# Two up blocks ahead of the q sums and the router in a fused attention and expert kernel

## The chip, the cores and the metric

The kernel runs on one core of a Trainium2 chip. The metric is the device time of one launch in microseconds (us), median of the runs; lower is better.

## The reference

A transformer block over 32 batch elements of 256 tokens, width 256, in float32. First comes attention with 4 heads of 64: queries from the normalized tokens, keys and values from the tokens and 77 context rows, so 333 keys. Then comes a mixture of experts on the result, with a shared part of inner width 512 and 8 experts of inner width 128, of which a router picks two per token.

```python
x = x + attention(ctx, layernorm(x), mask)     # q and k are divided by their RMS per head
h = layernorm(x)
logits = h @ gate_weight.T                     # sigmoid, bias, best of two groups, top 2 of 8, weights sum to 2.5
routed = sum over experts e of w[t, e] * (relu(h @ up[e].T) ** 2) @ down[e].T
shared = (relu(h @ shared_up.T) ** 2) @ shared_down.T
x = x + routed + shared
```

## The kernel before, in words

Every engine has its program written out by hand, in a function `step(b, experts, following)` that is run for the 32 batch elements; engines meet through semaphores that count up. Step b does the attention of element b and, woven into it, the expert part of element b-1 (`f`), and towards its end it projects k, v and q of element b+1. The first step has no expert part, the last one no next element (`following` is false), and after the loop the expert part of element 31 runs alone.

Precision: a float32 product is made of three float32r matmuls, from a high and a low part of either operand (`split_product`, L295 to L297). So each activation is copied once rounded (hi, mostly ScalarE) and subtracted once (lo, VectorE or GpSimd).

**TensorE** (step from L512 on): `transpose_k` (six transposes, L362), `sum_q_squares` (L349: 32 small matmuls in four column tiles into bank 0 of `attn_ps`), `router` (L465: 32 of the same kind into bank 3 of `attn_ps`), `up` 0 and 1 (L295 to L297, 12 matmuls each), the first two score pairs (L383 to L387, two at a time on half of the rows), `up` 2 and 3, score pairs 2 and 3, the shared down block (24 matmuls), transposes of probabilities 0 to 2 (L397, three each), then expert down blocks, `up` 4 and 5, and further transposes in turn. At the end come the projections of b+1, `down` 6, the four transposes of x2 (L452), and `down` 7.

PSUM has eight banks: four in `attn_ps`, two in `up_ps` (up blocks take turns), two in `down_ps` (shared part and experts take turns). Heads u and u+4 share a bank of `attn_ps`; transposed probabilities 0 to 2 go to banks 0 to 2, so `transpose_probs(b, u)` waits until head u+4 has been masked out of its bank:

```python
if u < PT_RING:
    pe.wait_ge(masked_done, b * U + SCORE_RING + u + 1)
```

**VectorE** in one step: `k_low` twice, statistics of the input of b+1, `mask_scores` of heads 0 to 3 (L906), `negate_max` (L913, 128x4, needs `q_scale`), the first eight levels of the router's choice (L996 to L1017: small operations, each waiting for the one before; `pair_hi` L1003, `top2` L1010, `group_sum` L1012, the two `group_sel` L1015 and L1017), `mask_scores` of heads 4 to 7, further levels, the shared sum (L1058), casts of hidden pairs 3 to 5 (L1052) between the accumulations of the experts (L1067). Near the end: `normalize2` (L968), `k_norms` and `k_normalize` of b+1, `x2_low` (L976), `q_low`, `add(6)`, `q_norms` (L864), `add(7)`.

**ScalarE**: `k_high`, `router_exp` (the exponential of the logits), then `hidden(p)` for up pairs 0 to 2 (relu out of PSUM, square as high part, square as float32), the softmax exponentials, copies out of PSUM; at the end `q_out` (copy and square of q) and `x2_high` (x2 as float32 and as high part).

**GpSimd** in one step, in this order: `q_scales` (a power operation on 128x8), `hidden_low` 0 to 2 (L1268, a 128x512 subtraction of two SBUF tensors each), `rstd_first` (a power operation on 128x3; not in the first and last steps), `residual` (L1242, x_res, a 128x512 addition of two SBUF tensors), `hidden_low` 3 and 4, `ln_low`, `hidden_low` 5, `rstd_second`, `k_scales`.

SP issues the loads of b+2, which wait for x_hat and x_res of b, and the stores.

Of the kernel before, what the change touches and what calls it, by code (L numbers as in the profile page):

```python
# [33 lines left out]
def build(nc, x, ctx_in, mask, vectors, w_q, w_kv, w_out, b_out, gate_t, gate_bias, up_t, down_t, out):  # L34
# [21 lines left out]
    with ExitStack() as stack:  # L56
# [234 lines left out]
        def _(pe):  # L291
# [48 lines left out]
            def sum_q_squares(b, first):  # L340


                pe.wait_ge(q_sq_done, b + 1)
                if first:
                    pe.wait_ge(head_sel_done, 1)
                for t in range(T):
                    for ft in range(FT):
                        for tile in COLUMN_TILES:
                            last = nc.tensor.matmul(attn_ps[tile, 0, t * H + 2 * ft:t * H + 2 * ft + 2],  # L349
                                                    q_sq[:, ft, t * P + tile.start:t * P + tile.stop], head_sel[:],  # L350
                                                    start=True, stop=True)
                last.then_inc(qn_ps, 1)
# [14 lines left out]
            def score_pair(b, pair, experts):  # L367
                t, ft = divmod(pair, FT)
                u = 2 * pair
                cols = slice(t * P, (t + 1) * P)  # L370
                if pair == 0:
                    pe.wait_ge(q_norm_done, b + 1)
                    pe.wait_ge(k_hi_done, (b + 1) * FT)
                    pe.wait_ge(k_lo_done, (b + 1) * FT)
                elif pair == 1:
                    if experts:
                        pe.wait_ge(exp_neg_done, b)
                else:
                    pe.wait_ge(masked_done, b * U + u - 2)
                low, high = slice(0, DH), slice(DH, P)  # L380
                banks = [attn_ps[:, (u + i) % SCORE_RING, 0:KPAD] for i in range(2)]
                for i, rows in enumerate((low, high)):
                    nc.tensor.matmul(banks[i], q_hi[rows, ft, cols], k_hi[rows, ft, :], start=True, stop=False)  # L383
                for i, rows in enumerate((low, high)):
                    nc.tensor.matmul(banks[i], q_hi[rows, ft, cols], k_lo[rows, ft, :], start=False, stop=False)
                for i, rows in enumerate((low, high)):
                    nc.tensor.matmul(banks[i], q_lo[rows, ft, cols], k_hi[rows, ft, :], start=False,  # L387
                                     stop=True).then_inc(score_ps, 1)
# [67 lines left out]
            def router(b, first):  # L456

                if first:
                    pe.wait_ge(gate_in, DMA)
                pe.wait_ge(x2_full_done, (b + 1) * FT)  # L460
                pe.wait_ge(x2_hi_done, (b + 1) * FT)
                for t in range(T):
                    for k in range(FT):
                        for tile in COLUMN_TILES:
                            last = nc.tensor.matmul(attn_ps[tile, 3, t * E:(t + 1) * E],  # L465
                                                    x2_full[:, k, t * P + tile.start:t * P + tile.stop],
                                                    gate_stage[:, k, :], start=k == 0, stop=k == FT - 1)
                last.then_inc(logit_ps, 1)

            def up(b, p, first, following=True):  # L470

                if first and p == 0:
                    pe.wait_ge(w_lo_done, 3 + QUART)
                if p == 0:
                    pe.wait_ge(x2_hi_done, (b + 1) * FT)
                    pe.wait_ge(x2_lo_done, (b + 1) * FT)
                if p == 1 and following:
                    pe.wait_ge(q_lo_done, b + 2)
                if p >= 2 or not first:
                    pe.wait_ge(relu_done, b * PAIRS + p - 1)  # L480
                for j in range(2):
                    for k in range(FT):
                        cols = slice((2 * p + j) * P, (2 * p + j + 1) * P)
                        last = split_product(up_ps[:, (p + 1) % 2, j * S:(j + 1) * S], (up_hi[:, k, cols], up_lo[:, k, cols]),
                                             (x2_hi[:, k, :], x2_lo[:, k, :]), k == 0, k == FT - 1)
                last.then_inc(up_done, 1)
# [6 lines left out]
            def down_shared(b, t, first):  # L493
                if first and t == 0:
                    pe.wait_ge(down_lo_done, QUART)
                if t == 0:
                    pe.wait_ge(*hid_hi_ready(b, SP_PAIRS - 1))
                    pe.wait_ge(hid_lo_done, b * PAIRS + SP_PAIRS)
                    if not first:
                        pe.wait_ge(acc_done, b * ACC)  # L500
                for f in range(FS):
                    last = split_product(down_ps[:, 0, t * D:(t + 1) * D], hidden(f, t),
                                         (down_hi[:, f, :], down_lo[:, f, :]), f == 0, f == FS - 1)
# [3 lines left out]
            def down_expert(b, e, first):  # L507
# [3 lines left out]
                if e > 0:  # L511
                    pe.wait_ge(acc_done, b * ACC + 2 * e - 1)  # L512
                elif not first:
                    pe.wait_ge(acc_done, b * ACC - 2)
                for t in range(T):
# [4 lines left out]
            def step(b, experts, following):  # L520
# [11 lines left out]

                transpose_k(b)
                sum_q_squares(b, first)
                if experts:
                    router(f, f_first)
                ffn("up", 0)
                ffn("up", 1)
                score_pair(b, 0, experts)
# [48 lines left out]
                project_kv(b + 1, 0)  # L588
                project_q(b + 1)
                ffn("down", 6)  # L590
                transpose_x2(b)
                ffn("down", 7)
# [13 lines left out]
            steps(step)  # L606
            router(B - 1, False)
            up(B - 1, 0, False, False)
            up(B - 1, 1, False, False)
            up(B - 1, 2, False)  # L610
            up(B - 1, 3, False)
# [11 lines left out]
        def _(act):  # L623
# [15 lines left out]
            def q_out(b, first):  # L639
# [4 lines left out]
                qv = up_ps[:, 0, :].rearrange("p (f s) -> p f s", f=FT)  # L644
                nc.scalar.activation(q_hi[:], qv, ACT.Copy).then_inc(q_hi_done, 1)
                nc.scalar.activation(q_sq[:], qv, ACT.Square).then_inc(q_sq_done, 1)

# [63 lines left out]
            def router_exp(b, first):  # L711
                act.wait_ge(logit_ps, b + 1)
                if not first:
                    act.wait_ge(router_step, (b - 1) * ROUTER_STEPS + 1)
                nc.scalar.activation(exp_neg[:], attn_ps[:, 3, 0:T * E].rearrange("p (t e) -> p t e", t=T),
                                     ACT.Exp, scale=-1.0).then_inc(exp_neg_done, 1)
# [14 lines left out]
            def step(b, experts, following):  # L731
                first = isinstance(b, int) and b == 0
                f, f_first = b - 1, isinstance(b, int) and b == 1
                ffn = (lambda p: hidden(f, p, f_first)) if experts else (lambda p: None)
                k_high(b, first)
                if experts:
                    router_exp(f, f_first)
                ffn(0)
                if first:
# [29 lines left out]
                if following:  # L769
# [3 lines left out]
                    q_out(b + 1, False)  # L773
                x2_high(b, first)

            act.wait_ge(kv_in, DMA)
# [12 lines left out]
            v_out(0, 1, True)  # L789
            q_out(0, True)  # L790
            for cols in UP_COLS[1:]:
                split_hi(up_hi[:, :, cols], up_stage[:, :, cols])
            steps(step)
            router_exp(B - 1, False)
            hidden(B - 1, 0, False)
            for p in range(1, PAIRS):
# [4 lines left out]
        def _(dve):  # L801
# [57 lines left out]
            def q_norms(b, first):  # L859

                dve.wait_ge(qn_ps, b + 1)
                if not first:
                    dve.wait_ge(q_scale_done, b)
                nc.vector.tensor_scalar(q_norm[:], attn_ps[:, 0, 0:U], DH * RMS_EPS * RMS_EPS, None,  # L864
                                        ALU.max).then_inc(q_norm_done, 1)
# [105 lines left out]

            def x2_low(b):
                for ft in range(FT):
                    dve.wait_ge(x2_full_done, b * FT + ft + 1)
# [104 lines left out]
            def step(b, experts, following):  # L1079
# [15 lines left out]
                k_low(b, 0)  # L1095
                k_low(b, 1)
                if first:
                    normalize1(1, False)
                    up_parts(0)
# [66 lines left out]
                k_norms(b + 1, 1, False)  # L1166
                k_normalize(b + 1, 0, False)
                k_normalize(b + 1, 1, False)
                x2_low(b)
                q_low(b + 1)  # L1170
                add(6)
                q_norms(b + 1, False)
                add(7)

# [25 lines left out]
            q_low(0)  # L1200
            q_norms(0, True)
            dve.wait_ge(gamma_done, 1)
# [18 lines left out]
        def _(pool):  # L1221
# [49 lines left out]
            def step(b, experts, following):  # L1271
                first = isinstance(b, int) and b == 0

                def low(p):
                    if experts:
                        hidden_low(b - 1, p)

                q_scales(b, first)
                if first:
                    for i, rows in enumerate(DOWN_ROWS):  # L1280
                        pool.wait_ge(w_hi_done, 4 + QUART + i)
                        nc.gpsimd.tensor_tensor(down_lo[:, rows, :], down_stage[:, rows, :], down_hi[:, rows, :],
                                                ALU.subtract).then_inc(down_lo_done, 1)
                low(0)
                low(1)
# [75 lines left out]
```

## Time and profile before

| what | value |
|---|---|
| median of 3 runs | 1172.76 us (1172.66 to 1172.81) |
| the profiled execution, its own time | 1171.52 us |
| its span, first to last instruction | 1169.7 us |
| TensorE matmul busy | 1145.7 us (98%) |
| VectorE busy | 1006.4 us (86%) |
| ScalarE busy | 801.6 us (69%) |
| GpSimd busy | 555.2 us (47%) |
| mean granted TensorE clock | 0.993 of full speed |

Busy is the share of the span in which an engine has an instruction in execution. Matmuls overlap, so the starts of two matmuls, not their durations, tell what one costs in a row of them. In the timeline a row gives the start, the duration, engine, line, operation, the tiles written and read, and their sizes; x9 means nine instructions merged, and a bracket at the end tells how long the engine stood idle before the row and for whom. An operation that has begun but is held shows as a long duration, not as idle time.

### The profile page before, as it was taken

Reading aid. Unit: us, or ns where it says so; the run is one execution under the profiler, and the core shown is the slowest. Engines: PE = TensorE matmul, PEld = TensorE weight load, DVE = VectorE, ACT = ScalarE, POOL = GpSimd, SP = SyncE. Lnnn points to the kernel's source line nnn. Section 1 sums busy time; section 2 is a strip of 40 time slices with the busy share of each in tenths; the row PEclk is TensorE's granted clock in tenths of the full one; section 3 lists DMA queues with packets and bytes.
Section 4 is the critical chain, followed back from the end, with each engine's and each line's share of the span. In section 5 each row is a group of like instructions: output and inputs, shape, how many; then the busy total and the mean of one; then the engine's idle time right before and its main releaser. Section 6 shows DMA issues by size and latency. Waiting matters only on the chain. (4 is left out here: it accounts for less than half of the span.)

```text
span 1169.7 us, 32985 instructions
## 1 busy us (share of the span) xinstructions
PE 1145.7 (98%) x11772; PEld 1070.1 (91%) x11772; DVE 1006.4 (86%) x3500; ACT 801.6 (69%) x1900; POOL 555.2 (47%) x473
## 2 busy tenths in 40 slices
PE   7799999999999999999999999999999999999997
PEld 6699999999999999999999999999999999999997
DVE  6688988889888889888899888899888899888877
ACT  5577766677766768766778666678666677666673
POOL 5445444445444445454445454444454444454442
PEclk8899999999999999999999999999999999999999
DMA  5000000000000000000000000000000000000000
GB/s 173 13 14 23 23 22 12 14 23 23 23 12 22 14 23 22 23 11 23 14 22 23 23 11 22 13 23 23 22 11 22 14 23 22 23 10 15 10 11 19
DMA packets 28145, 26.06 MB, mean 22 GB/s; under 512 B 6544, under 2 KB 27440, under 8 KB 27984
## 3 DMA queue, kind: packets, MB, share of 16 engines
q1 hardware_dynamic: 27904, 23.83, 6.5%
q8 instruction: 95, 1.56, 0.6%
q14 instruction: 66, 0.54, 0.2%
q0 software_dynamic: 80, 0.14, 0.1%
HBM read 15.57 MB, written 8.39 MB: 20 GB/s over the span
## 5 line engine op out<-in xcount | busy, mean ns | idle before, releaser
L1268 POOL TENSOR_TENSOR hid_lo<-relu,hid_hi 128x512 fp32r<-128x512 f32 x192 | 248.3, 1293 | 246.6 <-DVE hid_hi L1052 166.2
L295 PE MATMUL down_ps<-down_hi,hid_hi 128*128 128x256 f32 x768 | 233.6, 304 | 1.7 <-ACT hid_hi L726 1.0
L1067 DVE SCALAR_TENSOR_TENSOR acc<-down_ps,route_w,acc 128x256 f32<-128x256 f32 x512 | 222.0, 475 | 8.9 <-PE down_ps L297 8.2
L295 PE MATMUL up_ps<-x_hi,up_hi 128*128 128x256 f32 x768 | 226.8, 295 | 0.0
L297 PE MATMUL down_ps<-down_hi,hid_lo 128*128 128x256 f32 x768 | 215.9, 281 | 0.0
L296 PE MATMUL down_ps<-down_lo,hid_hi 128*128 128x256 f32 x768 | 215.7, 281 | 0.0
L296 PE MATMUL up_ps<-x_lo,up_hi 128*128 128x256 f32 x768 | 214.3, 279 | 0.0
L297 PE MATMUL up_ps<-x_hi,up_lo 128*128 128x256 f32 x768 | 214.2, 279 | 0.0
L676 ACT ACTIVATE probs<-masked,neg_max,q_scale 128x333 f32<-128x333 f32 x256 | 168.1, 658 | 3.4 <-DVE neg_max L913 3.4
L721 ACT ACTIVATE relu_sb<-up_ps 128x512 f32<-128x512 f32 x192 | 113.6, 592 | 72.4 <-PE up_ps L297 69.1
L295 PEld LDWEIGHTS down_ps<-down_hi,hid_hi 128*128 128x128 f32 x768 | 144.4, 188 | 14.2 <-issue 12.9
L295 PEld LDWEIGHTS up_ps<-x_hi,up_hi 128*128 128x128 f32 x768 | 144.0, 188 | 7.3 <-ACT relu_sb L721 6.5
L296 PEld LDWEIGHTS down_ps<-down_lo,hid_hi 128*128 128x128 f32 x768 | 145.2, 189 | 0.0
L297 PEld LDWEIGHTS up_ps<-x_hi,up_lo 128*128 128x128 f32 x768 | 144.4, 188 | 0.0
L297 PEld LDWEIGHTS down_ps<-down_hi,hid_lo 128*128 128x128 f32 x768 | 144.4, 188 | 0.0
L296 PEld LDWEIGHTS up_ps<-x_lo,up_hi 128*128 128x128 f32 x768 | 144.2, 188 | 0.0
L1223 POOL TENSOR_TENSOR rstd<-var,minus_half 128x2 f32<-128x2 f32 (+1 forms) x64 | 49.9, 780 | 167.7 <-DVE var L961 165.7
L683 ACT ACTIVATE up_stage<-attn_ps 111x384 f32<-111x384 f32 x256 | 117.3, 485 | 16.9 <-PE attn_ps L397 16.9
L729 ACT ACTIVATE relu<-relu_sb 128x512 f32<-128x512 f32 x192 | 119.7, 624 | 3.0
L653 ACT ACTIVATE k_sq<-attn_ps 111x512 f32<-111x512 f32 x64 | 31.5, 492 | 125.6 <-PE attn_ps L297 125.6
L906 DVE CUSTOM_DVE_ANT_0 masked<-attn_ps,mask_row 128x333 f32<-128x333 f32 x256 | 114.0, 498 | 2.1 <-issue 2.1
L397 PE MATMUL attn_ps<-ident,probs 128*111 128x128 f32 x768 | 107.7, 277 | 7.0 <-DVE row_max L906 6.9
(145 smaller groups left out, 2851.1 us busy)
## 6 DMA issues: line engine op xcount, KB each, us to landing
out<-acc SPq DMA_DIRECT2D x31, 256.0 KB, 2.2
x_first<-in_x SPq DMA_DIRECT2D x16, 256.0 KB, 2.7
w_stage<-in_x SPq DMA_DIRECT2D x16, 256.0 KB, 2.8
up_stage<-in_up_t SPq DMA_DIRECT2D x1, 1536.0 KB, 6.8
down_stage<-in_down_t SPq DMA_DIRECT2D x1, 1536.0 KB, 8.5
c_first<-in_ctx SPq DMA_DIRECT2D x16, 77.0 KB
w_stage<-in_ctx SPq DMA_DIRECT2D x16, 77.0 KB
w_stage<-in_w_kv SPq DMA_DIRECT2D x1, 512.0 KB, 4.1
```

Of the source, the lines that this page charges most:

```text
L295: nc.tensor.matmul(out_ap, s_hi, m_hi, start=first, stop=False)
L296: nc.tensor.matmul(out_ap, s_hi, m_lo, start=False, stop=False)
L297: return nc.tensor.matmul(out_ap, s_lo, m_hi, start=False, stop=last)
L397: last = nc.tensor.transpose(attn_ps[0:KC, u % PT_RING, c * P:(c + 1) * P], probs[:, u, c * KC:(c + 1) * KC], ident[:])
L676: nc.scalar.activation(probs[:, u, :], masked[:, u, :], ACT.Exp, bias=neg_max[:, u:u + 1], scale=q_scale[:, u:u + 1], accum_out=row_sum[:, ...
L683: nc.scalar.activation(probs_t[:, u % PT_SB, :], attn_ps[0:KC, u % PT_RING, 0:CH * P], ACT.Copy).then_inc(pt_done, 1)
L721: nc.scalar.activation(relu_sb[:, p % 2, :], up_ps[:, (p + 1) % 2, :], ACT.Relu).then_inc(relu_done, 1)
L729: nc.scalar.activation(relu2[:, p % 2, :], relu_sb[:, p % 2, :], ACT.Square).then_inc(relu2_done, 1)
L906: nc.vector.tensor_tensor_reduce(masked[:, u, :], attn_ps[:, u % SCORE_RING, 0:KEYS], mask_row[:], 1.0, -MASKED, ALU.add, ALU.max, row_max ...
L1067: nc.vector.scalar_tensor_tensor(acc[:, t, :], down_ps[:, (e + 1) % 2, t * D:(t + 1) * D], route_w[:, t, e:e + 1], acc[:, t, :], ALU.mult, ...
L1223: nc.gpsimd.tensor_tensor(dst, src, minus_half[0:src.shape[0], 0:src.shape[1]], ALU.pow).then_inc(done, 1)
L1268: nc.gpsimd.tensor_tensor(hid_lo[:, p % HID_RING, :], relu2[:, p % 2, :], hid_hi[:, p % HID_RING, :], ALU.subtract).then_inc(hid_lo_done, 1)
```

## The change

On TensorE, `up` 0 and 1 go ahead of the q sums and the router, so that these two stand directly before score pairs 0 and 1. The q sums now write bank 0 of `down_ps`, the logits bank 1, and both wait until the accumulations of the element before have read those banks. The wait of score pair 0 on `q_norm` goes, and so does that of score pair 1 on `exp_neg`; the shared down block waits for `q_norm` instead and expert 0 for `exp_neg`. The transposes of x2 move ahead of `down` 6. `up` 0 waits for the first half of x2_lo, and for the second half at its fourth matmul.

On ScalarE the square of q moves behind `x2_high`, and `router_exp` behind `hidden(0)`. On VectorE the first half of `x2_low` moves between the two `k_normalize`, and `q_norms` from the end of a step to behind `k_low` of the next. On GpSimd `hidden_low(0)` moves ahead of `q_scales`. The closing stage after the loop takes the same order of router and up blocks. No arithmetic is added or removed.

```diff
@@ sum_q_squares
                 if first:
                     pe.wait_ge(head_sel_done, 1)
+                elif b > 1:
+                    pe.wait_ge(acc_done, (b - 1) * ACC)
...
-                            last = nc.tensor.matmul(attn_ps[tile, 0, t * H + 2 * ft:t * H + 2 * ft + 2],
+                            last = nc.tensor.matmul(down_ps[tile, 0, t * H + 2 * ft:t * H + 2 * ft + 2],
@@ score_pair
                 if pair == 0:
-                    pe.wait_ge(q_norm_done, b + 1)
                     pe.wait_ge(k_hi_done, (b + 1) * FT)
                     pe.wait_ge(k_lo_done, (b + 1) * FT)
-                elif pair == 1:
-                    if experts:
-                        pe.wait_ge(exp_neg_done, b)
-                else:
+                elif pair > 1:
                     pe.wait_ge(masked_done, b * U + u - 2)
@@ router
                 if first:
                     pe.wait_ge(gate_in, DMA)
+                else:
+                    pe.wait_ge(acc_done, b * ACC)
...
-                            last = nc.tensor.matmul(attn_ps[tile, 3, t * E:(t + 1) * E],
+                            last = nc.tensor.matmul(down_ps[tile, 1, t * E:(t + 1) * E],
@@ up
-                    pe.wait_ge(x2_lo_done, (b + 1) * FT)
+                    pe.wait_ge(x2_lo_done, b * FT + 1)
...
+                        if p == 0 and j == 0 and k == 1:
+                            pe.wait_ge(x2_lo_done, (b + 1) * FT)
@@ down_shared
                     if not first:
                         pe.wait_ge(acc_done, b * ACC)
+                    if b + 1 < B:
+                        pe.wait_ge(q_norm_done, b + 2)
@@ down_expert
-                elif not first:
-                    pe.wait_ge(acc_done, b * ACC - 2)
+                else:
+                    pe.wait_ge(exp_neg_done, b + 1)
@@ TensorE step
                 transpose_k(b)
+                ffn("up", 0)
+                ffn("up", 1)
                 sum_q_squares(b, first)
                 if experts:
                     router(f, f_first)
-                ffn("up", 0)
-                ffn("up", 1)
                 score_pair(b, 0, experts)
...
                 project_q(b + 1)
+                transpose_x2(b)
                 ffn("down", 6)
-                transpose_x2(b)
                 ffn("down", 7)
...
-            router(B - 1, False)
             up(B - 1, 0, False, False)
             up(B - 1, 1, False, False)
+            router(B - 1, False)
@@ ScalarE
                 nc.scalar.activation(q_hi[:], qv, ACT.Copy).then_inc(q_hi_done, 1)
+
+            def q_square(b):
+                qv = up_ps[:, 0, :].rearrange("p (f s) -> p f s", f=FT)
                 nc.scalar.activation(q_sq[:], qv, ACT.Square).then_inc(q_sq_done, 1)
...
                 k_high(b, first)
+                ffn(0)
                 if experts:
                     router_exp(f, f_first)
-                ffn(0)
...
                 x2_high(b, first)
+                if following:
+                    q_square(b + 1)
@@ VectorE step
                 k_low(b, 0)
                 k_low(b, 1)
+                q_norms(b, first)
...
                 k_normalize(b + 1, 0, False)
+                x2_low(b, 0)
                 k_normalize(b + 1, 1, False)
-                x2_low(b)
+                x2_low(b, 1)
                 q_low(b + 1)
                 add(6)
-                q_norms(b + 1, False)
                 add(7)
@@ GpSimd step
+                low(0)
                 q_scales(b, first)
...
-                low(0)
                 low(1)
                 low(2)
```

## Rows read from the trace of the kernel before

**Rows 1.** Timeline of TensorE's matmuls, one steady step.

```profile
512.12 0.38 PE L452 MATMUL attn_ps<-ident,x_hat 128*128 128x128 f32 x2
...
513.28 0.75 PE L362 MATMUL attn_ps<-ident,k_rms 111*128 111x111 f32 x6
...
514.62 0.39 PE L295 MATMUL up_ps<-x_hi,up_hi 128*128 128x256 f32 x1
514.84 0.28 PE L296 MATMUL up_ps<-x_lo,up_hi 128*128 128x256 f32 x1
...
517.43 0.28 PE L297 MATMUL up_ps<-x_hi,up_lo 128*128 128x256 f32 x1
517.66 0.42 PE L383 MATMUL attn_ps<-k_hi,q_hi 64*128 64x334 f32 x2
...
525.90 1.14 PE L397 MATMUL attn_ps<-ident,probs 128*111 128x128 f32 x9
526.80 0.36 PE L295 MATMUL down_ps<-down_hi,hid_hi 128*128 128x256 f32 x1
527.00 0.28 PE L296 MATMUL down_ps<-down_lo,hid_hi 128*128 128x256 f32 x1
...
532.45 0.28 PE L295 MATMUL down_ps<-down_hi,hid_hi 128*128 128x256 f32 x1
```

**Rows 2.** Timeline of VectorE, the same step.

```profile
510.24 0.73 DVE L968 TENSOR_SCALAR x_hat<-x,mv,rstd 128x256 f32<-128x256 f32 x2
...
515.70 0.87 DVE L1067 SCALAR_TENSOR_TENSOR acc<-down_ps,route_w,acc 128x256 f32<-128x256 f32 x2
...
520.59 0.66 DVE L913 SCALAR_TENSOR_TENSOR neg_max<-row_max,q_scale 128x4 f32<-128x4 f32 x1
...
522.00 0.17 DVE L1003 TENSOR_TENSOR pair_hi<-biased 128x8 f32<-128x8 f32 x1
...
522.62 1.14 DVE L1010 TENSOR_TENSOR top<-mid_a,mid_b 128x4 f32<-128x4 f32 x1
523.79 0.16 DVE L1012 TENSOR_TENSOR group_sum<-top 128x4 f32<-128x4 f32 x1
523.99 0.16 DVE L1015 TENSOR_TENSOR group_sel<-group_sum 128x2 f32<-128x2 f32 x1
...
524.15 0.50 DVE L906 CUSTOM_DVE_ANT_0 masked<-attn_ps,mask_row 128x333 f32<-128x333 f32 x1
```

**Rows 3.** Timeline of GpSimd, the same step.

```profile
515.87 1.64 POOL L1223 TENSOR_TENSOR q_scale<-q_norm,minus_half 128x8 f32<-128x8 f32 x1 [2.75 <-DVE q_norm L864]
518.26 1.30 POOL L1268 TENSOR_TENSOR hid_lo<-relu,hid_hi 128x512 fp32r<-128x512 f32 x1 [0.76 <-ACT relu L729]
519.94 1.30 POOL L1268 TENSOR_TENSOR hid_lo<-relu,hid_hi 128x512 fp32r<-128x512 f32 x1 [0.37 <-ACT relu L729]
522.42 1.32 POOL L1268 TENSOR_TENSOR hid_lo<-relu,hid_hi 128x512 fp32r<-128x512 f32 x1 [1.19 <-ACT relu L729]
523.70 0.85 POOL L1223 TENSOR_TENSOR rstd<-var,minus_half 128x3 f32<-128x3 f32 x1
524.52 1.29 POOL L1242 TENSOR_TENSOR x_res<-x_first,bout_row 128x512 f32<-128x512 f32 x1
530.37 1.28 POOL L1268 TENSOR_TENSOR hid_lo<-relu,hid_hi 128x512 fp32r<-128x512 f32 x1 [4.56 <-DVE hid_hi L1052]
```

**Rows 4.** Timeline of VectorE, the last step of the loop.

```profile
1123.52 1.21 DVE L1012 TENSOR_TENSOR group_sum<-top 128x4 f32<-128x4 f32 x1
...
1124.92 0.50 DVE L906 CUSTOM_DVE_ANT_0 masked<-attn_ps,mask_row 128x333 f32<-128x333 f32 x1
```

**Rows 5.** Timeline of GpSimd, the last step of the loop.

```profile
1123.43 1.29 POOL L1242 TENSOR_TENSOR x_res<-w_stage,bout_row 128x512 f32<-128x512 f32 x1
```

**Rows 6.** Timeline of TensorE's matmuls, the last step of the loop.

```profile
1125.65 1.33 PE L397 MATMUL attn_ps<-ident,probs 128*111 128x128 f32 x9
1126.74 0.37 PE L295 MATMUL down_ps<-down_hi,hid_hi 128*128 128x256 f32 x1
```

More of the change, by code:

```diff
@@ L714, in router_exp @@
                     act.wait_ge(router_step, (b - 1) * ROUTER_STEPS + 1)
-                nc.scalar.activation(exp_neg[:], attn_ps[:, 3, 0:T * E].rearrange("p (t e) -> p t e", t=T),
+                nc.scalar.activation(exp_neg[:], down_ps[:, 1, 0:T * E].rearrange("p (t e) -> p t e", t=T),
                                      ACT.Exp, scale=-1.0).then_inc(exp_neg_done, 1)
@@ L790, in _ @@
             q_out(0, True)
+            q_square(0)
             for cols in UP_COLS[1:]:
@@ L793, in _ @@
             steps(step)
+            hidden(B - 1, 0, False)
             router_exp(B - 1, False)
-            hidden(B - 1, 0, False)
             for p in range(1, PAIRS):
@@ L863, in q_norms @@
                     dve.wait_ge(q_scale_done, b)
-                nc.vector.tensor_scalar(q_norm[:], attn_ps[:, 0, 0:U], DH * RMS_EPS * RMS_EPS, None,
+                nc.vector.tensor_scalar(q_norm[:], down_ps[:, 0, 0:U], DH * RMS_EPS * RMS_EPS, None,
                                         ALU.max).then_inc(q_norm_done, 1)
@@ L970, in normalize2, with x2_low @@
                 last.then_inc(x2_hat_done, 1)
-            def x2_low(b):
-                for ft in range(FT):
+            def x2_low(b, *parts):
+                for ft in parts or range(FT):
                     dve.wait_ge(x2_full_done, b * FT + ft + 1)
@@ L1200, in _ @@
             q_low(0)
-            q_norms(0, True)
             dve.wait_ge(gamma_done, 1)
```

## The prediction

> **What bounds the kernel now.** Start with the table of engines: TensorE is busy 98% of the span, VectorE 86%, ScalarE 69%, GpSimd 47%. So TensorE's own sequence is the clock of the kernel, and a change pays only if it shortens that sequence without making TensorE wait. Read next the timeline of TensorE in one steady step. From the transposes of k to the first score pair it never stands still; what it loses are breaks between kinds of matmul. From the second matmul of the two up blocks to their last, 22 starts take 517.43 - 514.84 = 2.59 us, 0.118 each; but the first two starts lie 0.22 apart, the first score matmul starts 0.23 after the last up matmul, and after transposes an up matmul follows without a delay of its own (nine in 0.90, 0.10 each) and its second matmul 0.20 later [rows 1]. Each break thus costs about 0.1. Last, read VectorE against GpSimd: there the kernel is much tighter than the busy shares say.
>
> **What the change removes on TensorE.** Before, from the start of the k transposes (513.28) to the first score (517.66) it is 4.38 us [rows 1]. Call the break from transposes into the small q-sum matmuls e; it has no row of its own. Six transposes at 0.10 are 0.60, so q sums, router and the break out of them are 514.62 - 513.28 - 0.60 - e = 0.74 - e. After: 0.60 of transposes, 24 up matmuls in 0.20 + 23 x 0.118 = 2.91, a break of 0.11 from up into q sums (as up into score, 0.23 - 0.12), then 0.74 - e with the break out of the router now falling on the score pair. Sum 4.36 - e. The saving is 0.02 + e. I take e = 0.11, the nearest row being the break from up into score; its ends are 0 and 0.22 (twice that break). **Saving 0.12 us a step, 0.02 to 0.24**; over 31 steps with both score pairs and experts 3.7 us.
>
> **The moved work that stays covered.** The transposes of x2 change places with one down block of six matmuls: 0.71 earlier, 512.12 becomes 511.41. x2_hat ended at 510.24 + 0.73 = 510.97 [rows 1, 2], 0.44 before: nothing, and if that slack were gone the wait would fall on TensorE directly, with a down block queued behind it. Up 0 starts 513.88 instead of 514.62; for it ScalarE copies x2 before it squares q, VectorE makes the first half of x2_lo between the two normalizations of k, and the second half is asked for three matmuls (0.35) later. The slack of these has no row, so it stands in the bound below. The new wait of q sums and router on acc: expert 7's accumulations end at 515.70 + 0.87 = 516.57 [rows 2] even in the old order, with q_norm ahead of them; q sums now start after both up blocks, near 516.9. Nothing; were it late, both score pairs would queue behind it. The waits of the shared down block on q_norm and of expert 0 on exp_neg concern values that are read before the masking of the same step begins. SP's queue issues the same loads; the one that waits for x_res moves by a tenth. Bounds for all of these together: -0.05 to +0.15 us a step, taken as 0.
>
> **What gets late instead: GpSimd's queue, and through it VectorE.** Row by row: VectorE's tiny neg_max (128x4) took 0.66 us and ended at 521.25, just behind the hid_lo subtraction of pair 1, 519.94 + 1.30 = 521.24; `top2` (also 128x4) took 1.14 and ended at 523.76, behind hid_lo of pair 2 at 523.74; `group_sum`, of the same size, 0.16 [rows 2, 3]. A VectorE operation with two SBUF tensors stands until such a GpSimd subtraction is done. In the last step, where x_res follows hid_lo at once, `group_sum` itself took 1.21 us, started 0.09 after x_res and ended with it [rows 4, 5]: x_res (128x512) does the same. The power operation rstd does not: `group_sum` started 0.09 after it and took 0.16 [rows 2, 3].
>
> Now the change puts hid_lo of pair 0 *ahead* of q_scale. Up 1 started at 514.62 + 0.22 + 11 x 0.118 = 516.14; it will start at 513.88 + 0.20 + 1.30 = 515.38, 0.76 earlier, and hid_lo 0 with it: 518.26 becomes 517.50. But behind it come 1.30 + 1.64 (q_scale) + 1.30 without a gap (neighbours overlap by some 0.04), so hid_lo 1 ends at about 521.70 instead of 521.24 [rows 3]. neg_max needs q_scale, so it always meets hid_lo 1: it ends **0.45 later**, and everything behind it on VectorE moves: `pair_hi` from 522.00 to 522.45. hid_lo 2 follows TensorE: 522.42 - 0.12 = 522.30. So it now catches `pair_hi`, not `top2`: that ends at 522.30 + 1.32 + 0.02 = 523.64, with more of the router's chain still to do. From the end of `pair_hi` (522.17) to the first `group_sel` is 0.45 to `top2`, 0.16 for it unheld, 0.03, and 0.20: 0.84 [rows 2]. So `group_sel` comes at 524.48. x_res starts 2.10 after hid_lo 2: at 524.40. It has the port by 0.08 us, as it had by 0.09 in the last step, and the second `group_sel` is later still. Both end behind x_res, 525.71; the masking of score pair 2, which starts as the first `group_sel` ends, moves from 524.15 to 525.71: **1.56 late**.
>
> **What that costs TensorE.** The transposes of probabilities 0 to 2 need the masking of heads 4 to 6 out of the banks. In the steady step masking started 1.75 before the nine transposes and they took 0.90 [rows 1, 2]; in the last step it started 0.73 before them (1124.92 against 1125.65) and they took 1.09: 0.19 of stall [rows 4, 6]. After the change it starts at 525.71, the transposes want to start at 525.78: a lead of 0.07, so the stall is 0.19 + 0.66 = **0.85**. In the timeline VectorE shows no idle time from there to its cast for hid_hi 3, so hid_lo 3 ends at 530.37 + 1.28 + 1.56 = 533.21 [rows 3]; the down block of expert 2 would start at 532.45 - 0.12 + 0.85 = 533.18 [rows 1]: with the hand-over another 0.1. Later in the step VectorE waits for TensorE again, so the lateness is not carried over. Sum: -0.12 + 0.85 + 0.10 = **+0.83 us a step**. It holds for the 30 steps that have rstd between hid_lo 2 and x_res: 24.9. In the last step x_res already struck; neg_max's 0.45 is most of what is new there: +0.4. The closing stage moves the router behind up 1, while VectorE has idle time before the shared sum: 0. Total +25.3: 1171.52 of the profiled execution becomes 1196.8. The median of the runs is 1.24 above it, so 1172.76 + 25.3 = **1198**. With the saving between 0.02 and 0.24, the stall 0.55 to 1.05 and 0 to 0.2 for expert 2, a step costs +0.4 to +1.15, so 1185 to 1207.
>
> Here a rule of the Trainium skill goes further than the rows. SBUF — State Buffer, section "Who interferes with whom", says that a VectorE instruction with two SBUF inputs contends with any GpSimd instruction that reads SBUF, and that the later one blocks fully. The trace agrees for the subtractions and the addition, but not for the power operation, which reads SBUF too: 0.16 for `group_sum` inside rstd; the measurement decides.
>
> **The rivals.**
> - *Escape, faster.* All hangs on 0.08 us at `group_sel` and 0.16 at its second half. If hid_lo 1 ends 0.2 earlier, or hid_lo 2 starts 0.2 later, more of the chain is done before the hold, both `group_sel` run free under rstd, masking comes no more than some 0.6 late, a lead of about 1.0, and TensorE does not wait. For it: the difference is small, and GpSimd's rows are rough. Against it: the steps repeat, and the last step shows what happens at 0.09. Then 31 x 0.12 = 3.7 less: 1169, ends 1165 and 1172. Chance 0.17.
> - *The joined visit saves nothing, and escape.* The break from the router's small matmuls into the half-height score matmuls has no row; at twice 0.11 the saving is gone. The longer visit delays hid_lo 2, which helps the escape: 1171 to 1175. Chance 0.07.
> - *Power operations hold VectorE too.* Then rstd holds the operation behind `pair_lo` until x_res starts, and x_res holds it on: of the 1.00 between the end of `pair_hi` and the masking (0.84 + 0.16) some 0.7 then still follow 525.71, by estimate, and 30 x 0.7 = 21 more: 1219. Against it: `group_sum` under rstd, in 30 steps alike. This is the rule above taken whole. Chance 0.03.
> - *Other stalls*: x2's transposes or q sums wait a little at the head of the step though `group_sel` escapes: up to 0.3 a step, 1176 to 1182. Chance 0.05.
>
> **How the numbers follow.** The hold by x_res has 0.68; with the power operations and the other stalls slower has 0.76. About 0.2% (2.3 us) is what a measurement can tell from no change: same 0.07, faster 0.17. The likeliest case alone has 1185 to 1207. To hold 8 in 10 the range must also take in the escape, so 1166 to 1207; cases of both signs are inside it.
>
> **What would show it.** Right: in the profile after, neg_max ends near 0.45 later relative to TensorE, `pair_hi` takes over 1 us in place of `top2`, a `group_sel` takes over 1 us under x_res, the nine transposes of probabilities wait for row_max in every step, for 0.8 us or so, and the visit with q sums, router and scores has one break fewer. Wrong: if `group_sel` stays at 0.16 us, or if it is held and the transposes still take 0.90, because the probabilities' path has slack that the last step does not show.

## The result and the profile after

The changed kernel takes 1213.64 us (median of 4 runs, 1212.66 to 1216.34), the kernel before 1172.71 (median of 4, 1172.66 to 1172.81): a ratio of 1.0353, 95% interval 1.0335 to 1.0371. It is slower, as forecast, but by 40.9 us instead of 25.3, and so outside the forecast range, which ended at 1207. The profiled execution after took 1214.38 us with a span of 1212.6, at a mean granted TensorE clock of 0.993, the same as before.

First the table of engines after, one line of the page:

```profile
PE 1170.0 (96%) x11772; PEld 1079.2 (89%) x11772; DVE 1025.4 (85%) x3500; ACT 805.6 (66%) x1900; POOL 551.4 (45%) x473
```

No work was added (the counts of these five engines are those of before), yet TensorE's busy time grew by 24.3 us and VectorE's by 19.0: an instruction that has begun and is held counts as busy. So the shares can't say where the time went; the view of waits and the timelines can. Two waits of TensorE and one of VectorE from that view, the engine that waits first, behind the arrow what it waited for (total us, times, longest):

```profile
PE attn_ps L395 <- DVE row_max L916: 19.3, 32, 7.0
PE down_ps L295 <- DVE acc L1077: 7.4, 34, 0.3
DVE attn L944 <- issue: 60.7, 30, 2.0
```

Before, the first was a single wait of the prologue (6.9 us, once), the second 0.7 us in 3 waits, all of them behind the loop, and the third was 30.2 us in 30 waits of 1.0. So the view names two places where the step became longer: the transposes of probabilities and a down block that waits for an accumulation of an expert. Behind the masking, VectorE now has its first idle time at line 944, 2.03 us where it was 1.01. Before, it had an earlier one, behind expert 2's accumulation, where it waited for the down block of expert 3:

```profile
534.70 0.88 DVE L1067 SCALAR_TENSOR_TENSOR acc<-down_ps,route_w,acc 128x256 f32<-128x256 f32 x2 [0.26 <-PE down_ps L297]
```

Now one steady step after. Add 18.42 to a time of after to lay it over the step shown of before: then the transposes of k start together, 494.86 + 18.42 = 513.28 [rows 1]. The timeline of TensorE:

```profile
494.86 0.79 PE L364 MATMUL attn_ps<-ident,k_rms 111*128 111x111 f32 x6
495.42 0.36 PE L295 MATMUL up_ps<-x_hi,up_hi 128*128 128x256 f32 x1
...
498.22 0.28 PE L297 MATMUL up_ps<-x_hi,up_lo 128*128 128x256 f32 x1
498.42 0.43 PE L351 MATMUL down_ps<-head_sel,q_sq 128*32 128x2 f32 x32
...
499.07 0.42 PE L381 MATMUL attn_ps<-k_hi,q_hi 64*128 64x334 f32 x2
...
507.87 1.41 PE L395 MATMUL attn_ps<-ident,probs 128*111 128x128 f32 x9 [0.40 <-DVE row_max L916]
509.03 0.37 PE L295 MATMUL down_ps<-down_hi,hid_hi 128*128 128x256 f32 x1
...
514.83 0.36 PE L295 MATMUL down_ps<-down_hi,hid_hi 128*128 128x256 f32 x1
515.03 0.28 PE L296 MATMUL down_ps<-down_lo,hid_hi 128*128 128x256 f32 x1
...
516.96 0.49 PE L395 MATMUL attn_ps<-ident,probs 128*111 128x128 f32 x3
517.67 0.36 PE L295 MATMUL down_ps<-down_hi,hid_hi 128*128 128x256 f32 x1 [0.22 <-DVE acc L1077]
```

The head of the step is one uninterrupted row of matmuls, and its first score starts at 499.07 + 18.42 = 517.49 instead of 517.66: the change does what it says, 0.17 us a step. Then the step falls behind: by 0.65 behind the nine transposes (509.03 + 18.42 = 527.45 against 526.80), by 0.80 at expert 2's down block (533.25 against 532.45), and by 1.35 at expert 4's. Expert 2's block waits for its low part, which GpSimd made at 513.43 to 514.73. The last place is not in the rows ahead of the prediction, so here it is in the kernel before, TensorE's timeline and then VectorE's:

```profile
534.50 0.49 PE L397 MATMUL attn_ps<-ident,probs 128*111 128x128 f32 x3
534.74 0.37 PE L295 MATMUL down_ps<-down_hi,hid_hi 128*128 128x256 f32 x1
```

```profile
533.57 0.86 DVE L1067 SCALAR_TENSOR_TENSOR acc<-down_ps,route_w,acc 128x256 f32<-128x256 f32 x2
```

Three transposes are followed after 0.24 by expert 4's down block, with no wait. It writes the bank of `down_ps` that expert 2 used, and so needs expert 2's accumulation, which ended at 533.57 + 0.86 = 534.43. After, those 0.24 are 517.67 - 516.96 = 0.71: 0.47 of stall.

VectorE and GpSimd in the same step after:

```profile
502.18 1.02 DVE L923 SCALAR_TENSOR_TENSOR neg_max<-row_max,q_scale 128x4 f32<-128x4 f32 x1
...
503.95 1.19 DVE L1013 TENSOR_TENSOR pair_hi<-biased 128x8 f32<-128x8 f32 x1
...
505.25 0.16 DVE L1016 TENSOR_TENSOR top<-pair_hi 128x4 f32<-128x4 f32 x1
...
505.79 0.16 DVE L1022 TENSOR_TENSOR group_sum<-top 128x4 f32<-128x4 f32 x1
505.99 1.23 DVE L1025 TENSOR_TENSOR group_sel<-group_sum 128x2 f32<-128x2 f32 x1
...
507.22 0.49 DVE L916 CUSTOM_DVE_ANT_0 masked<-attn_ps,mask_row 128x333 f32<-128x333 f32 x1
...
516.66 1.65 DVE L1077 SCALAR_TENSOR_TENSOR acc<-down_ps,route_w,acc 128x256 f32<-128x256 f32 x4
```

```profile
499.05 1.29 POOL L1278 TENSOR_TENSOR hid_lo<-relu,hid_hi 128x512 fp32r<-128x512 f32 x1 [4.36 <-ACT relu L736]
500.29 1.64 POOL L1233 TENSOR_TENSOR q_scale<-q_norm,minus_half 128x8 f32<-128x8 f32 x1
501.89 1.29 POOL L1278 TENSOR_TENSOR hid_lo<-relu,hid_hi 128x512 fp32r<-128x512 f32 x1
503.83 1.28 POOL L1278 TENSOR_TENSOR hid_lo<-relu,hid_hi 128x512 fp32r<-128x512 f32 x1 [0.65 <-ACT relu L736]
505.07 0.86 POOL L1233 TENSOR_TENSOR rstd<-var,minus_half 128x3 f32<-128x3 f32 x1
505.91 1.29 POOL L1252 TENSOR_TENSOR x_res<-w_stage,bout_row 128x512 f32<-128x512 f32 x1
```

Read the two together by their ends. `neg_max` ends at 503.20 with hid_lo of pair 1 (503.18), `pair_hi` at 505.14 with hid_lo of pair 2 (505.11), `group_sel` at 507.22 with x_res (507.20). A VectorE operation on two elements per partition took 1.23 us because x_res started 0.08 before it. By lines, over all 32 steps (ns: least, median, most), `group_sel` is held in the steady case, and `group_sum`, which begins inside rstd, never:

```profile
L1025 DVE TENSOR_TENSOR group_sel<-group_sum x32: 160/1227/1231, 66.3 to 1197.5; 128x2 f32<-128x2 f32 x32
```

```profile
L1022 DVE TENSOR_TENSOR group_sum<-top x32: 161/161/163, 66.1 to 1197.3; 128x4 f32<-128x4 f32 x32
```

From one rstd on 128x3 to that of the second step behind it (505.07 to 578.30) it is 2 x 36.62 us after, and 35.27 from one to the next before: 1.35 a step, and over 30 steps 40.5 of the 40.9 us.

### The profile page after: what moved, and what is told of

It reads as the page before. It is cut to its first block and busy times, and to the rows that moved or that the text cites. A ratio compares the mean times of both kernels' runs of the same rounds, so it can differ in the third digit from the quotient of the medians.

```text
span 1212.6 us, 33046 instructions
## 1 busy us (share of the span) xinstructions
PE 1170.0 (96%) x11772; PEld 1079.2 (89%) x11772; DVE 1025.4 (85%) x3500; ACT 805.6 (66%) x1900; POOL 551.4 (45%) x473
## 3 DMA queue, kind: packets, MB, share of 16 engines
q8 instruction: 95, 1.56, 0.5%
## 5 line engine op out<-in xcount | busy, mean ns | idle before, releaser
L1077 DVE SCALAR_TENSOR_TENSOR acc<-down_ps,route_w,acc 128x256 f32<-128x256 f32 x512 | 216.8, 473 | 1.3 <-PE down_ps L297 0.7
L395 PE MATMUL attn_ps<-ident,probs 128*111 128x128 f32 x768 | 115.0, 283 | 19.8 <-DVE row_max L916 19.3
L395 PEld LDWEIGHTS attn_ps<-ident,probs 128*111 128x111 f32 x768 | 97.5, 178 | 29.5 <-issue 25.2
```

The source lines that it names most:

```text
L395: last = nc.tensor.transpose(attn_ps[0:KC, u % PT_RING, c * P:(c + 1) * P], probs[:, u, c * KC:(c + 1) * KC], ident[:])
L1077: nc.vector.scalar_tensor_tensor(acc[:, t, :], down_ps[:, (e + 1) % 2, t * D:(t + 1) * D], route_w[:, t, e:e + 1], acc[:, t, :], ALU.mult, ...
```

## The experiments

Three questions were open. Does the hold of `group_sel` by x_res carry the loss, or is it the matmuls moved on TensorE with their new waits? Does `hidden_low(0)` ahead of `q_scales` bring it about? And what is the second wait, that for an accumulation? The theory at the start was that this second wait only follows from the first.

**x_res behind hid_lo of pair 4, in the changed kernel and in the kernel before.** The same edit in both, so that what x_res's place is worth by itself is seen too. Here and below a cut shows the moved lines, with `...` where lines are left out.

```diff
                     rstd_first(b + 1, False)
-                residual(b, first)
                 low(3)
                 low(4)
+                residual(b, first)
```

> The changed kernel with one edit: GpSimd makes x_res behind hid_lo 4 instead of behind rstd. Theory of the hold (hid_lo 1 late, neg_max late, then x_res catches group_sel): neg_max still ends about 0.4 us late, but group_sel takes 0.16 again, masking of score pair 2 starts some 1.1 us before the nine transposes, they take 0.90, and all three waits of TensorE go. What is left is the shorter sequence on TensorE, 0.17 us a step: 1172.7 - 5 = 1167.5. Rival of the new waits and the new order on TensorE itself: x_res is nothing to it, 1213. Rival that the late neg_max and the hold of pair_hi are enough: most of the loss stays, over 1195.

> The kernel before with the same one edit (x_res behind hid_lo 4), as a control. In it x_res runs beside the masking, which it does not hold, so nothing is freed but in the last step (0.2 us): theory 1172.5, the same within 0.1%. If x_res in its new place held VectorE's copies (inv_wide, ln_hi) so that TensorE waits, it would be slower by 0.2 us a step or more, 1179, and then the run of the changed kernel with this edit is slower by as much.

Measured: the changed kernel with this edit takes 1180.94 us (median of 6 runs, 1180.17 to 1182.90), ratio 1.0065 to the kernel before (interval 1.0051 to 1.0078); the kernel before with it takes 1172.94 (12 runs), ratio 0.9997 (0.9988 to 1.0006). So x_res's place is worth nothing in the kernel before and 32.7 us in the changed one: the hold is the greater part of the loss. But the changed kernel was to come out at 1167.5 and stays 13 above that. The first `group_sel` over all steps, a wait, GpSimd and TensorE of the changed kernel with x_res late:

```profile
L1025 DVE TENSOR_TENSOR group_sel<-group_sum x32: 160/160/161, 66.1 to 1164.6; 128x2 f32<-128x2 f32 x32
```

```profile
PE down_ps L295 <- DVE acc L1077: 7.0, 34, 0.3
```

```profile
527.80 0.87 POOL L1233 TENSOR_TENSOR rstd<-var,minus_half 128x3 f32<-128x3 f32 x1
...
563.36 0.86 POOL L1233 TENSOR_TENSOR rstd<-var,minus_half 128x3 f32<-128x3 f32 x1
```

```profile
530.03 1.15 PE L395 MATMUL attn_ps<-ident,probs 128*111 128x128 f32 x9
530.93 0.36 PE L295 MATMUL down_ps<-down_hi,hid_hi 128*128 128x256 f32 x1
...
538.63 0.49 PE L395 MATMUL attn_ps<-ident,probs 128*111 128x128 f32 x3
539.33 0.36 PE L295 MATMUL down_ps<-down_hi,hid_hi 128*128 128x256 f32 x1 [0.20 <-DVE acc L1077]
```

The nine transposes take 0.90 again, without a wait, but expert 4's down block comes 0.70 behind its transposes instead of 0.24. A step is 35.56 long: 0.17 less at its head and 0.46 more here, 0.29 over the 35.27 of before. So the theory fell in one point: the second wait does not follow from the first. It stays when VectorE is late only by `neg_max`'s 0.37 and TensorE 0.17 early. (x_res in its new place starts 0.42 behind the second widening copy, which takes 0.61 as before, so it is not x_res that makes VectorE late here.)

**x_res a quarter of a microsecond later, in its old place of the order.** If the 0.08 us at `group_sel` decide, a small filler on GpSimd, which writes a new tile `spare` that nobody reads, must bring back as much as moving x_res past two subtractions.

```diff
                     rstd_first(b + 1, False)
+                nc.gpsimd.memset(spare[:], 0.0)
                 residual(b, first)
```

> The changed kernel with a filler of some 0.25 us on GpSimd (a 128x256 constant written to an unused tile) between rstd and x_res, so that x_res starts behind both group_sel instead of 0.08 us ahead of the first. Theory: group_sel takes 0.16 again, masking is only 0.4 us late; the transposes and expert 2 do not wait, expert 4 still waits for the sum of expert 2 by some 0.45: a step 0.29 us longer than before, as with x_res moved behind hid_lo 4: 1181, range 1178 to 1184. Rival that x_res's place mattered in the earlier run for another reason than group_sel's start: 1205 to 1220.

Measured: 1181.74 us (median of 4, 1180.98 to 1184.75), ratio 1.0089 (1.0072 to 1.0106). Work was added, and 31.9 us went. GpSimd's and VectorE's timelines:

```profile
527.60 0.86 POOL L1234 TENSOR_TENSOR rstd<-var,minus_half 128x3 f32<-128x3 f32 x1
528.41 0.30 POOL L1300 MEMSET spare<- 128x256 f32 x1
528.68 1.29 POOL L1253 TENSOR_TENSOR x_res<-x_first,bout_row 128x512 f32<-128x512 f32 x1
```

```profile
528.51 0.16 DVE L1026 TENSOR_TENSOR group_sel<-group_sum 128x2 f32<-128x2 f32 x1
528.59 0.15 DVE L1028 TENSOR_TENSOR group_sel<-group_sum 128x2 f32<-128x2 f32 x1
528.67 0.50 DVE L917 CUSTOM_DVE_ANT_0 masked<-attn_ps,mask_row 128x333 f32<-128x333 f32 x1
```

Both `group_sel` get through, the first of them inside the filler, which only writes; x_res then runs beside the masking, which is not held.

**The kernel before, with one part of the new GpSimd order, and with an early x_res.** First only `hidden_low(0)` ahead of `q_scales`:

```diff
+                low(0)
                 q_scales(b, first)
...
-                low(0)
                 low(1)
```

> The kernel before with one part of the change alone: on GpSimd hid_lo 0 goes ahead of q_scale; TensorE, ScalarE and VectorE stay as they were. Theory of the hold: the old TensorE order gives hid_lo 0 later, so q_scale and hid_lo 1 come later still; neg_max ends about 1.2 us late, hid_lo 2 follows at once, group_sum or group_sel is held by x_res, masking of pair 2 starts near 1.9 us late, and the wait of the down block of expert 4 for the sum of expert 2 makes the step about 1.7 us longer: 1172.7 + 52 = 1225, range 1210 to 1235. Rival of the TensorE order and its new waits: this queue order alone costs nothing, 1173.

Then only x_res ahead of rstd, which has it follow hid_lo 2 at once and strike `group_sum`:

```diff
                 low(2)
+                residual(b, first)
                 if following and not first:
                     rstd_first(b + 1, False)
-                residual(b, first)
```

> The kernel before with one edit that makes x_res hold the router's chain on purpose: on GpSimd x_res goes ahead of rstd, right behind hid_lo 2, as it lies in the last step. Everything else as before. Theory: group_sum takes 1.2 us in every step, masking of pair 2 starts 1.0 us late; the nine transposes take 1.09 (0.19 of stall), and with VectorE 1.0 late the down block of expert 4 waits for the sum of expert 2, so that the step is 0.8 us longer in all: 1172.7 + 24 = 1197, range 1185 to 1203. If only the stall at the transposes counts, 0.19 a step: 1178.5. Rival that the hold by x_res is harmless without the new order: 1173.

One execution each: 1230.59 us and 1202.36 us, beside 1173.21 for the kernel before. Neither moves a matmul or a bank, and the first alone costs 57 us, more than the whole change. `group_sum` by lines in the first and in the second of them:

```profile
L1012 DVE TENSOR_TENSOR group_sum<-top x32: 161/1199/1207, 68.0 to 1207.6; 128x4 f32<-128x4 f32 x32
```

```profile
L1012 DVE TENSOR_TENSOR group_sum<-top x32: 161/1218/1226, 67.3 to 1179.4; 128x4 f32<-128x4 f32 x32
```

In the kernel before it has 164 ns as its median. Their waits of TensorE, the early x_res last:

```profile
PE attn_ps L397 <- DVE row_max L906: 31.2, 32, 6.9
PE down_ps L295 <- DVE acc L1067: 7.3, 33, 0.3
```

```profile
PE down_ps L295 <- DVE acc L1067: 7.2, 33, 0.3
```

In the second kernel `group_sum` is held without anything late before it, and the wait for the accumulation appears with its 7 us all the same: here too a lateness of VectorE ends in it. In the first the new TensorE order is missing, so hid_lo of pair 0 starts later, and q_scale behind it too: VectorE there stood idle 0.69 for q_scale before `neg_max` began. So in the change the earlier up blocks seem to soften the cost of the GpSimd order that came with them; no run shows the two apart in the changed kernel.

**Expert 2's accumulation ahead of the second widening of the inverse sums.** What VectorE does just before that accumulation is a reciprocal (0.16) and a copy of 128x256 (0.62 in the step of after) that TensorE asks for later than the accumulation. Changing their order frees the bank earlier and touches neither the hold nor the transposes. This takes the second wait by itself.

```diff
                 add(1)
+                if following:
+                    add(2)
                 invert_sums(b, 1)
                 widen_inverse(b, 1, first)
...
-                add(2)
                 add(3)
```

> The changed kernel with one edit on VectorE: the accumulation of expert 2 goes ahead of the second inverse and its widening, 0.75 us of work earlier; GpSimd as in the change, so x_res still holds group_sel. Theory of three waits (0.82 at the nine transposes, 0.21 at the down block of expert 2, 0.47 at the down block of expert 4, less 0.17 saved = 1.35 a step, where only the first two were forecast): the third goes, 30 x 0.47 = 14 less: 1213.6 - 14 = 1199.5, range 1196 to 1203. Rival that VectorE's lateness comes out at TensorE at a later place all the same (the transposes of the inverse sums): 1208 to 1214.

Measured: 1199.96 us (median of 4, 1199.76 to 1202.28), ratio 1.0240 (1.0226 to 1.0254); the kernel before beside it had 1172.98. The view of waits has 19.4 us in 32 waits for row_max, nearly as after (19.3), and for acc only 0.8 us in 4 waits (before: 0.7 in 3). So the second wait is worth 13.7 us, and what is left, 27.0 over before, is what the prediction had summed up (25.3).

**Both edits, and x_res still later.** First the two together, with x_res behind hid_lo 4, then with x_res behind hid_lo 5, past the widening; last that second pair of edits in the kernel before.

> The changed kernel with both edits: x_res behind hid_lo 4, and expert 2's accumulation ahead of the second inverse. Theory: no wait of the three is left, the shorter TensorE sequence shows at last: 0.17 x 31 = 5 less than before: 1168. The second widening of the inverse now comes late and beside x_res, which holds it; if TensorE's transposes of the inverse wait for it by 0.1 to 0.3, 1171 to 1177. Rival that VectorE, 0.45 late from neg_max on, stays the bound at another place: 1180.

> As the run before, but x_res behind hid_lo 5, where GpSimd is idle for 5 us and the widening of the inverse is over. Theory: 1168, and not slower than the run before; the subtractions for at_lo may be held by x_res for up to 0.3 us, then 1170 to 1177. Rival that VectorE's 0.45 is the bound elsewhere: 1180.

> The kernel before with the two edits of the last run (x_res behind hid_lo 5, expert 2's accumulation ahead of the second inverse), as its control. Theory: in the kernel before none of the three waits is there, so the edits free nothing but the 0.2 us in the last step: 1172.7, the same within 0.1%; what the last run gained is then the shorter TensorE sequence of the change. Rival that the edits gain by themselves and the change nothing: 1169.5.

| kernel | median us | ratio to before (95%) |
|---|---|---|
| changed, x_res behind hid_lo 4, expert 2 first | 1171.85 | 0.9991 (0.9983 to 1.0000) |
| changed, x_res behind hid_lo 5, expert 2 first | 1169.45 | 0.9972 (0.9963 to 0.9981) |
| before, x_res behind hid_lo 5, expert 2 first | 1173.10 | 0.9999 (0.9990 to 1.0009) |

The middle one beats both kernels, by 3.5 us and 44.2, and as the same edits give the kernel before nothing, its gain is the change's own shorter row of matmuls. A step of it, from GpSimd's rstd, and TensorE's waits for row_max, of which only the prologue's is left (for acc it has four, 0.8 us together):

```profile
522.38 0.86 POOL L1234 TENSOR_TENSOR rstd<-var,minus_half 128x3 f32<-128x3 f32 x1
...
557.50 0.86 POOL L1234 TENSOR_TENSOR rstd<-var,minus_half 128x3 f32<-128x3 f32 x1
```

```profile
PE attn_ps L395 <- DVE row_max L916: 7.0, 1, 7.0
```

35.12 against 35.27: 0.15 a step. The first kernel of the table has 2.4 us less of a gain because x_res there strikes the widening copy: TensorE's transposes of the inverse, which need this copy, start 0.05 behind its end and take 0.59 to the next kind of matmul instead of 0.53, and the step is 35.19. VectorE and GpSimd, first kernel, then VectorE in the second:

```profile
536.33 1.07 DVE L936 COPY inv_wide<-row_inv 128x256 f32<-128x256 f32 x1
```

```profile
535.97 1.28 POOL L1253 TENSOR_TENSOR x_res<-x_first,bout_row 128x512 f32<-128x512 f32 x1
```

```profile
533.15 0.29 DVE L936 COPY inv_wide<-row_inv 128x256 f32<-128x256 f32 x1
```

The copy reads one SBUF tensor, and it stands under x_res too: 1.07 instead of 0.29, ended 0.15 behind x_res.

## Why the prediction was wrong in size

Its direction was right, and so was the mechanism of the hold; a third place where it is paid was missing. Per step, in us, with times of after moved by 18.42:

| step of the prediction | forecast | measured |
|---|---|---|
| saving at the head of TensorE's step | -0.12 | -0.17 |
| stall of the nine transposes | +0.85 | +0.82 |
| expert 2's down block (wait, and a break at its second matmul) | +0.10 | +0.15 and +0.08 |
| expert 4's down block | 0 | +0.47 |
| sum | +0.83 | +1.35 |

**The head.** The saving was 0.02 + e, with e, the break into the q sums, taken as 0.11 between 0 and 0.22. It did have a row of its own in the kernel before:

```profile
513.97 0.43 PE L349 MATMUL attn_ps<-head_sel,q_sq 128*32 128x2 f32 x32
```

The q sums began 0.69 behind the start of the transposes of k; after, with the up blocks behind them, the six transposes take 0.56 and not the 0.60 of the sum, so e is 0.13. From the first up matmul to what stands behind the two blocks it is 3.00 instead of 3.04, which is the other 0.04 of the 0.17. That the joined visit saves nothing did not come true, nor did a stall at the head of the step: the up blocks start at 495.42, 0.56 behind the start of the transposes of k, and run without a gap, and the timeline names no wait there for acc, q_norm or x2_lo. What was costed at nothing there costs nothing.

**The chain on VectorE and GpSimd.** The working came within 0.08 us everywhere (forecast in brackets): `neg_max` ends 0.37 later (0.45); hid_lo 2 starts at 522.25 (522.30); `pair_hi` starts at 522.37 (522.45) and ends at 523.56 (523.64); `group_sel` comes at 524.41 (524.48), x_res at 524.33 (524.40), the masking at 525.64 (525.71), which is 1.49 late (1.56). `group_sel` and x_res both follow from the end of hid_lo 2 and shifted by the same 0.07, so the difference that decides, 0.08 between them, came out exactly. That it fell on this side is luck as well as working: the filler of a quarter of a microsecond shows how near the other case was.

**The rivals.** *Escape* fell: `group_sel` took 1227 ns in the median. It was a real rival, though: with the filler it came about, and even then the kernel stayed slower than before by 0.9%, because the wait at expert 4's block remains; its 1169 would not have come. *Power operations hold VectorE too* fell: `group_sum` never took over 163 ns, and `top` in the step shown lies wholly inside rstd (505.07 to 505.93) and took 0.16. The rule of the Trainium skill, SBUF — State Buffer, section "Who interferes with whom", agrees with the subtractions and the addition of this kernel and not with its power operations, after as before.

**The step that failed** is one sentence: "Later in the step VectorE waits for TensorE again, so the lateness is not carried over." The first half is true, the second does not follow from it: it depends on where VectorE waits first. Behind the masking that is expert 3's accumulation (the row of 534.70), so nothing takes its lateness of some 1.5 us back before expert 2's accumulation is done. Two down blocks of TensorE depend on what VectorE does up to there. Expert 2's was costed; expert 4's, which needs the bank that expert 2's accumulation frees, was put at nothing. Expert 2's accumulation ended at 534.43 before and ends at 516.66 + 0.83 (half of the four) + 18.42 = 535.91 after, 1.48 later; the down block is 1.35 later, so before it had some 0.13 to spare. Only behind that does the lateness shrink: expert 3's accumulation follows at once, and the cast of hid_hi 5 takes 0.41 instead of 1.12, so that expert 4's accumulation starts only 0.33 late (519.05 + 18.42 = 537.47 against 537.14). 30 steps of 0.47 are 14.1 us; the run that takes this wait away alone gave back 13.7. The terms of the range lacked it as well, hence 1207 as the upper end.

**What is open.** `neg_max` still ends 0.4 later in all these versions, since q_scale lies between two subtractions; an order in which it comes as early as before was not tried. The small break at the second matmul of expert 2's block (0.20 in place of 0.12) follows the wait there; that it is caused by it was only seen in the timeline, not tested.

## What to carry to other kernels

Follow a lateness of an in-order engine to the first idle time that it had before the change, and ask at every hand-over up to there how much slack it has; two hand-overs checked and a third left out cost 14 us here. Before moving work on one engine, look at which operations on its neighbours then overlap: the order on GpSimd, on no critical path and 45% busy, decided, with one move on VectorE, between 3.5% slower and 0.3% faster. A change that is right but moves others' timing may need these others moved too, and a control with the same moves in the old kernel tells whose gain it is.

## What the runs showed of the hardware

A VectorE operation that reads two SBUF tensors and no PSUM, and starts inside a 128x512 subtraction or addition on GpSimd, 0.08 us or more behind its start in the rows shown, stands until that is done; the small ones here (128x2 to 128x8) end 0.02 to 0.03 us behind it (128x2: 0.16 us free, 1.23 held). A copy with one SBUF tensor does so too: 0.29 us free, 1.07 when it starts 0.36 behind x_res, and 0.61 in the kernel before, where it starts at 533.04 under hid_lo 4 (to 533.51). The Trainium skill, SBUF — State Buffer, section "Who interferes with whom", says that copies can contend with GpSimd when they run in a mode that uses two ports; these rows agree, and the mode is not seen in them. It does not happen at every start inside: in the changed kernel the cast of hid_hi 5 (128x512, one SBUF tensor) starts at 518.71, 0.08 behind a 128x333 subtraction on GpSimd, and takes 0.41, while in the kernel before it starts 0.20 behind one and takes 1.12. A power operation on GpSimd (128x3) and a memset (128x256) held nothing here, nor did x_res hold the masking, which reads PSUM and one SBUF tensor (0.50).
